# Layer 0's stacking transfers of a fused attention and expert kernel, split over two issuing engines

## The chip, the cores and the metric

The kernel runs on one core of one Trainium2 chip. Its engines are TensorE (PE), VectorE (DVE), ScalarE (ACT), GpSimd (POOL) and the sync engine (SP), each with a queue of its own that it takes in order; 16 DMA engines move data. The metric is the device time of one execution in microseconds; lower is better.

## The reference

Two layers on x (4 batches of 256 tokens, 128 wide) with a context (4 batches of 512 tokens, 96 wide). Each has cross-attention and a feed-forward part, both added to x after a layer norm. Layer 0's attention has 8 heads of 64:

```python
q = (x @ Wq).reshape(B, S, HEADS, DIM_HEAD).transpose(0, 2, 1, 3)
k = (context @ Wk).reshape(B, L, HEADS, DIM_HEAD).transpose(0, 2, 1, 3)
v = (context @ Wv).reshape(B, L, HEADS, DIM_HEAD).transpose(0, 2, 1, 3)
attn = jnp.einsum('bhsd,bhld->bhsl', q, k) * scale
attn = jax.nn.softmax(attn, axis=-1)
out = jnp.einsum('bhsl,bhld->bhsd', attn, v)
```

Its feed-forward part uses a fixed-point, piecewise linear gelu. Layer 1 has attention with 16 heads of 8 and a mixture of 8 experts, of which each token uses two.

## The kernel before, in words

Layer 0's attention goes batch by batch. Scores need near float32 accuracy at float16 speed, so each operand is kept as a high float16 part and a low one. For batch b, TensorE makes the projected keys (four matmuls "k0", one for each pair of heads) and queries ("q0", two) into banks of p_misc. ScalarE copies the high part into kx or qx (L1018, L1037), VectorE subtracts it from the bank for the low part (L755, L760) and gives the bank back. Each of kx and qx has one copy only, both parts of a batch beside each other.

Two heads lie one above the other in kx and qx. So that one matmul sums over 128 rows, "stack0" (L1250) moves them by transfers from SBUF to SBUF into kA, qA, kB and qB, views of a tile called region which have two buffers (b % 2): kA holds a head's high and low keys, qA its high queries twice, kB the high keys and qB the low queries. A batch takes six transfers of keys (256 KB each) and six of queries (128 KB each). The sync engine issues all twelve, in turn k k q q k k q q k q k q. It waits first for the keys' banks, before the first query transfer for the queries' banks, and from batch 2 on for the end of the scores of two batches back, whose buffer it overwrites. Each transfer adds 16 to one of kA_landed, qA_landed (one for even heads, one for odd), kB_landed, qB_landed.

Then TensorE makes "max" (a head's scores for its maximum, L468, reduced by VectorE at L766), "rows" (maxima transposed, L399, copied by ScalarE into mrow at L995, then by VectorE into qB at L780), "sc" (scores again, with the maxima taken off, L498; ScalarE's exponential at L1056 in two halves, each of which gives a bank back to the next head's scores) and "av" (values times probabilities, L517). "v0" is the projection of values, copied by ScalarE at L995; "ln", "xn" and "xT" are a layer norm's statistics, its result (VectorE, L729) and its transpose (TensorE, L399).

Before ScalarE overwrites kx or qx with the next batch, the old one must have left. It waits by stacked (L1003), which asks for all twelve transfers, in front of a batch's first key copy and its first query copy, and once more for layer 1, which uses kx and qx too.

The order of all steps is written out by schedule() (L65) as one list. Each engine walks the list and does its part of every kind that it knows; a kind that it doesn't know it passes. Around the change the list reads (kind, then batch and part or head; "stack0", b stands once for every batch):

- batch 0: q0 0 0, q0 0 1, **stack0 0**, split_w 1 (the weights' cast by ScalarE at L1001, the low part by VectorE at L744), cT 1, ln, v0 0 0, v0 0 1, xn, init 1, v0 0 2, v0 0 3, cT 2, cT 3, xT, max 0 0, k0 1 0, max 0 1, k0 1 1, ...
- batch 1: sc 0 1, max 0 5, q0 1 1, sum, max 0 6, **stack0 1**, sc 0 2, max 0 7, sum, init, sc 0 3, rows, k0 2 0, sum, av, max 1 0, k0 2 1, sc 0 4, sum, k0 2 2, ...
- batch 2: sc 0 7, max 1 5, sum, v0 1 0, av, max 1 6, ln, **stack0 2**, sc 1 0, v0 1 1, sum, max 1 7, av, rows, sc 1 1, v0 1 2, xT, xn, q0 3 0, ...
- batch 3: sc 1 7, y0, sum, av, max 2 6, **stack0 3**, sc 2 0, ln, sum, av, max 2 7, xn, sc 2 1, xT, up0, max 3 0, ...

Of the kernel before, what the change touches and what calls it, by code (L numbers as in the profile page):

```python
# [12 lines left out]
B = 4  # L13
# [213 lines left out]
def build(nc, t, out):  # L227
    ctx = ExitStack()
    with ctx:
        def sb(name, shape, dt=F32):  # L230
            return ctx.enter_context(nc.sbuf_tensor(name, shape, dt))

        def sem(name):
            return ctx.enter_context(nc.semaphore(name))

        def sems(name, n):
            return [sem(f"{name}{i}") for i in range(n)]
# [4 lines left out]
        cT = sb("cT", [CD, 2, B * C], F16)  # L242
# [22 lines left out]
        kA = region[:, 0:8192].rearrange("p (b h k) -> p b h k", b=2, h=H0)  # L265
        kB = region[:, 8192:16384].rearrange("p (b h k) -> p b h k", b=2, h=H0)
        qA = region[:, 16384:20480].rearrange("p (b h k) -> p b h k", b=2, h=H0)
        qB = region[:, 20480:24576].rearrange("p (b h k) -> p b h k", b=2, h=H0)
# [3 lines left out]
        kx = sb("kx", [P, 2, M0, C], F16)  # L272
        qx = sb("qx", [P, 2, M0, S], F16)
        v0 = sb("v0", [P, 2, KT, H0 * DH0])
# [8 lines left out]
        xT = sb("xT", [P, 2, S])  # L283
# [56 lines left out]
        kA_landed, qA_landed = sems("kA_landed", 2), sems("qA_landed", 2)  # L340
        kB_landed, qB_landed = sem("kB_landed"), sem("qB_landed")
# [3 lines left out]
        sc_full, sc_free = sems("sc_full", 2), sems("sc_free", 2)  # L345
# [25 lines left out]
        def misc_wait(eng, key):  # L371
            bank, use = misc[key]
            eng.wait_ge(misc_full[bank], use)
            return p_misc[:, bank, :], misc_free[bank]

        def misc_done(eng, key):

            bank, use = misc[key]
            eng.wait_ge(misc_free[bank], use)
# [3 lines left out]
        def head_number(layer, b, h):  # L383

            return b * H0 + h if layer == 0 else B * H0 + b * H1 + h
# [606 lines left out]
        def _(act):  # L992
# [7 lines left out]
                act.wait_ge(*((ld_wk0, 16) if n == 0 else (ld_wc, 48)))  # L1000
                act.copy(wc[:, 0, cols], wc_in[:, cols]).then_inc(wc_hi, 1)  # L1001

            def stacked(eng, batches):  # L1003
                for i in range(2):
                    eng.wait_ge(kA_landed[i], 32 * batches)
                    eng.wait_ge(qA_landed[i], 32 * batches)
                eng.wait_ge(kB_landed, 32 * batches)
                eng.wait_ge(qB_landed, 32 * batches)

            def context(b):  # L1010
                ps, _free = misc_wait(act, ("cT", b))
# [1 line left out]

            def keys0(b, m):
                if b and m == 0:
                    stacked(act, b)
                ps, _free = misc_wait(act, ("k0", b, m))
                act.copy(kx[:, 0, m, :], ps).then_inc(k_hi, 1)  # L1018

# [12 lines left out]

            def queries0(b, i):
                if b and i == 0:
                    stacked(act, b)
                ps, _free = misc_wait(act, ("q0", b, i))
                act.copy(qx[:, 0, 2 * i:2 * i + 2, :].rearrange("p m n -> p (m n)"), ps).then_inc(q_hi, 1)  # L1037

# [52 lines left out]
            def keys1(b):  # L1091

                if b == 0:
                    stacked(act, B)
                else:
                    act.wait_ge(k_bounced, 32 * b)
                ps, _free = misc_wait(act, ("k1", b))
                act.activation(kx[:, 0, 0, :], ps, ACT.Identity, bias=bk1[:, 0:1]).then_inc(k_hi, 1)

            def queries1(b):  # L1100
                if b == 0:
                    stacked(act, B)
                else:
                    act.wait_ge(q_bounced, 32 * b)
                ps, _free = misc_wait(act, ("q1", b))
                act.activation(qx[:, 0, 0, :], ps[:, 0:S], ACT.Identity, bias=bq1[:, 0:1]).then_inc(q_hi, 1)
# [9 lines left out]
            def activate(n, f):  # L1116
# [6 lines left out]
                if k:  # L1123
# [3 lines left out]
                    if last_n >= 2 and last_f == 0:  # L1127
                        act.wait_ge(y_full, last_n - 1)
                    act.copy(hh[:, last_n % 2, 0, last_f, :], hp[:, (k - 1) % 2, :]).then_inc(hh_done, 1)  # L1129

            steps = {"split_w": split_w, "cT": context, "k0": keys0, "v0": values0, "xT": xt, "q0": queries0, "rows": rows, "sc": softmax, "av": outputs,
                     "aT": heads_back, "up0": up0, "nodes": nodes_at, "k1": keys1, "q1": queries1, "aT1": heads_back1, "h1": up1,
                     "act": activate}
            for kind, *at in order:
# [98 lines left out]
        def _(sp):  # L1233
# [16 lines left out]
            def stack0(b):  # L1250


                def part(dst, src, i, low, landed):
                    sp.dma_start(dst[:, b % 2, i::2, :], src[64 * i:64 * i + 64, low, :, :]).then_inc(landed, 16)  # L1254

                for m in range(M0):
                    misc_done(sp, ("k0", b, m))
                if b >= 2:

                    sp.wait_ge(sc_full[1], head_number(0, b - 1, 0))  # L1260
                for i in range(2):
                    part(kA[0:64], kx, i, 0, kA_landed[i])
                    part(kA[64:128], kx, i, 1, kA_landed[i])
                    if i == 0:
                        for m in range(2):
                            misc_done(sp, ("q0", b, m))
                    part(qA[0:64], qx, i, 0, qA_landed[i])
                    part(qA[64:128], qx, i, 0, qA_landed[i])
                for i in range(2):
                    part(kB[0:64], kx, i, 0, kB_landed)  # L1270
                    part(qB[0:64], qx, i, 1, qB_landed)

            def bounce(b):

# [41 lines left out]
            def rest_of_weights(n):  # L1316
# [13 lines left out]
                sp.dma_start(f1b2[:, :], row(t["L1_xattn_b2"])).then_inc(ld_w2, 16)  # L1330

            steps = {"stack0": stack0, "zeros": zeros, "bounce": bounce, "stack1": stack1, "stage": stage_in, "init": rest_of_weights}
            for kind, *at in order:
                if kind in steps:
# [36 lines left out]
```

## Time and profile before

| | us |
|---|---|
| median of 3 runs | 501.96 (501.45 to 503.52) |
| the profiled execution | 501.99 |
| its span, first to last instruction | 500.3 |

| engine | busy us | share of the span |
|---|---|---|
| TensorE, matmuls | 436.3 | 87% |
| VectorE | 367.7 | 73% |
| ScalarE | 266.2 | 53% |
| GpSimd | 176.6 | 35% |

The mean granted clock of TensorE is 0.939 of full speed. The page also cuts the span into 40 equal slices of 12.5 us, each digit being tenths of a slice. Engines in the rows: PE is TensorE's matmul, PEld its weight load, DVE VectorE, ACT ScalarE, POOL GpSimd; SPq is the sync engine's queue, whose entries here are issues of transfers. Times count from the span's start. A timeline's row is: start, duration from the first to the last end of the merged instructions, engine, line, operation, output<-inputs, how many; in brackets the engine's idle time before it and what ended that. "p_misc L425" is a matmul of keys, and so on by the lines named above.

### The profile page before, as it was taken

How to read it: one execution, taken by the hardware profiler on the slowest of the kernel's cores; microseconds unless marked ns; L12 is line 12 of the kernel's file. 1: busy time of each engine (PE TensorE's matmuls, PEld its weight loads, DVE VectorE, ACT ScalarE, POOL GpSimd, SP SyncE). 2: the span in 40 equal slices, each digit the busy share in tenths (PEclk: the TensorE clock that was granted, in tenths of full speed). 3: DMA queues.
4: the chain of work that ended last, by engine and by line, in shares of the span. 5: the costliest groups of instructions: out<-in, count | busy, mean ns of one | idle time of the engine just before them, and what ended most of it. 6: DMA issues, size and time to landing. Idle time of an engine off the chain costs nothing.

```text
span 500.3 us, 8970 instructions
## 1 busy us (share of the span) xinstructions
PE 436.3 (87%) x3344; PEld 248.6 (50%) x3344; DVE 367.7 (73%) x718; ACT 266.2 (53%) x504; POOL 176.6 (35%) x205
## 2 busy tenths in 40 slices
PE   8569498997789968977985899999989999999996
PEld 3315154564356436544542544545546665656555
DVE  6855354555875799869986999882298888987775
ACT  3515253653824552456567376678755646465553
POOL 4218935427463492752426035710400104000000
PEclk9958698998979979997998899999999999999999
DMA  6664408007102005321142015400000000000000
GB/s 165 151 150 95 94 2 189 1 1 173 49 1 64 2 0 139 94 72 55 54 128 84 2 48 144 115 2 1 2 0 1 1 3 1 1 21 2 1 1 22
DMA packets 31487, 26.70 MB, mean 53 GB/s; under 512 B 4717, under 2 KB 28461, under 8 KB 31149
## 3 DMA queue, kind: packets, MB, share of 16 engines
q1 hardware_dynamic: 31445, 26.13, 20.9%
q8 instruction: 27, 0.44, 0.4%
q14 instruction: 15, 0.12, 0.1%
HBM read 12.10 MB, written 2.88 MB: 30 GB/s over the span
## 4 chain that ended last, share of the span: by engine, by line
PE 59%; DVE 22%; ACT 7%; issue 4%; SPq 3%; DMA 2%; POOL 2%; DVEq 0%; ACTq 0%; POOLq 0%
PE p_o L670 7%; PE p_sc L498 7%; PE p_misc L653 7%; PE p_sc L653 6%; PE p_misc L468 6%; DVE mx L766 6%; PE p_o L530 5%; PE p_o L517 4%; PE p_misc L399 4%; SPq L1254 3%; DVE xn L729 2%; DVE probs L953 2%; PE p_misc L425 2%; PE p_misc L562 2%; ACT probs L1122 2%
## 5 line engine op out<-in xcount | busy, mean ns | idle before, releaser
L766 DVE TENSOR_REDUCE mx<-p_misc 128x1 f32<-128x512 f32 x192 | 122.3, 684 | 20.4 <-PE p_misc L468 18.8
L1056 ACT ACTIVATE probs<-p_sc 128x512 f32<-128x512 f32 x192 | 104.6, 596 | 57.2 <-PE p_sc L498 56.9
L1122 ACT ACTIVATE probs<-p_misc 128x512 f32<-128x512 f32 x64 | 38.1, 597 | 56.6 <-PE p_sc L653 56.6
L953 DVE TENSOR_TENSOR probs<-probs,p_sc 128x512 f32<-128x512 f32 x64 | 44.0, 687 | 26.5 <-ACT probs L1122 24.7
L653 PE MATMUL p_misc<-qS,region 128*128 128x512 f16 x192 | 52.0, 380 | 3.8 <-DVE probs L953 2.6
L653 PE MATMUL p_sc<-qS,region 128*128 128x512 f16 x192 | 51.9, 379 | 0.0
L468 PE MATMUL p_misc<-kS,qS 96*128 96x512 f16 x128 | 40.6, 395 | 8.1 <-DVE mx L766 4.1
L1195 POOL TENSOR_TENSOR psums<-probs 128x256 f32<-128x256 f32 x32 | 26.0, 812 | 58.6 <-PE p_o L524 56.1
L1153 POOL TENSOR_SCALAR veps<-meanvar 128x2 f32<-128x2 f32 x16 | 3.7, 230 | 121.7 <-DVE meanvar L718 121.3
L670 PEld LDWEIGHTS p_o<-region,probs 128*128 128x128 f16 x720 | 42.7, 98 | 7.1
L670 PE MATMUL p_o<-region,probs 128*128 128x128 f16 x720 | 45.1, 219 | 0.0
L517 PE MATMUL p_o<-probs,v 128*64 128x256 f32 x256 | 38.3, 423 | 7.0 <-ACT probs L1056 7.0
L498 PE MATMUL p_sc<-qS,kS 128*128 128x256 f16 x256 | 40.6, 278 | 4.2 <-ACT probs L1056 3.9
L958 DVE TENSOR_TENSOR probs<-probs 128x512 f16<-128x512 f32 x64 | 43.8, 684 | 0.0
L530 PE MATMUL p_o<-probs,v 128*32 128x256 f32 x512 | 41.0, 398 | 0.0
L1129 ACT CAST probs<-probs 128x512 f16<-128x512 f32 x64 | 39.1, 611 | 1.4 <-DVE probs L953 1.4
L498 PE MATMUL p_sc<-region 128*128 128x256 f16 x256 | 36.6, 290 | 0.9 <-DVE region L780 0.9
L498 PEld LDWEIGHTS p_sc<-qS,kS 128*128 128x128 f16 x256 | 23.4, 98 | 19.8 <-ACT probs L1056 8.0
L498 PEld LDWEIGHTS p_sc<-region 128*128 128x128 f16 x256 | 25.7, 103 | 12.6 <-issue 3.6
L1213 POOL TENSOR_TENSOR region<-v,region 128x512 f16<-128x512 f32 x24 | 30.3, 1264 | 1.9
L653 PEld LDWEIGHTS p_sc<-qS,region 128*128 128x128 f16 x192 | 18.8, 98 | 22.7
L517 PEld LDWEIGHTS p_o<-probs,v 128*64 128x64 f32 x256 | 16.8, 146 | 24.7 <-issue 12.7
(163 smaller groups left out, 678.6 us busy)
## 6 DMA issues: line engine op xcount, KB each, us to landing
region<-kx SPq DMA_DIRECT2D x24, 256.0 KB, 3.9
v<-in_L_ffn_W_dram SPq DMA_DIRECT2D x24, 256.0 KB, 2.7
region<-qx SPq DMA_DIRECT2D x24, 128.0 KB, 3.9
kS<-kS SPq DMA_DIRECT2D x1, 1664.0 KB
kS<-k_scratch SPq DMA_DIRECT2D x8, 192.0 KB
k_scratch<-kx SPq DMA_DIRECT2D x4, 256.0 KB, 2.2
qS<-q_scratch SPq DMA_DIRECT2D x8, 96.0 KB
probs<-in_ctx_dram SPq DMA_DIRECT2D x1, 576.0 KB, 6.2
```

Source lines behind the costliest of these rows:

```text
L468: pe.matmul(ps, q[:, i * P:(i + 1) * P], k, start=True, stop=True).then_inc(full, 1)
L498: last = pe.matmul(p_sc[:, half, j * S:(j + 1) * S], k[:, kt * P:(kt + 1) * P], q, start=(i == 0), stop=(i == len(pairs) - 1))
L517: pe.matmul(p_o[64 * i:64 * i + 64, 0, m * S:(m + 1) * S], v0[:, b % 2, kt, h * DH0:(h + 1) * DH0], probs[:, h % 8, kt * S:(kt + 1) * S], ...
L530: last = pe.matmul(p_o[32 * j:32 * j + 32, n % 2, 0:S], v1[:, b % 2, c, h * VW:h * VW + 32], probs[:, h % 8, c * S:(c + 1) * S], start=(c ...
L653: last = pe.matmul(ps[:, f % 2, :], w[:, ws, e, f * P:(f + 1) * P], xh[:, xs, half * C:(half + 1) * C], start=(i == 0), stop=(i == 2))
L670: last = pe.matmul(p_o[:, n % 2, i * P:(i + 1) * P], hh[:, n % 2, hs, f, i * P:(i + 1) * P], ew[2][:, ws, e, f * P:(f + 1) * P], start=(at ...
L766: dve.tensor_reduce(mx[:, b % 2, i, h:h + 1], ps, AX_X, ALU.max).then_inc(free, 1)
L953: dve.tensor_tensor(hp[:, k % 2, :], sg[:, k % 2, :], p_sc[:, k % 2, :], ALU.mult).then_inc(hp_done, 1)
L958: dve.tensor_tensor(hh[:, n % 2, 1, f, :], hp[:, k % 2, :], hh[:, n % 2, 0, f, :], ALU.subtract).then_inc(hl_done, 1)
L1056: act.activation(probs[:, h % 8, half * 512:(half + 1) * 512], p_sc[:, half, :], ACT.Exp, scale=(DH0 if layer == 0 else DH1) ** -0.5).then ...
L1122: act.activation(sg[:, k % 2, :], p_misc[:, k % 2, :], ACT.Silu).then_inc(sg_done, 1)
L1129: act.copy(hh[:, last_n % 2, 0, last_f, :], hp[:, (k - 1) % 2, :]).then_inc(hh_done, 1)
```

## The change

The six query transfers of a batch are issued by ScalarE, at the place of "stack0" in ScalarE's own walk through the list, and the six key transfers still by the sync engine. ScalarE waits before them for the queries' two banks (VectorE's low parts), and from batch 2 on for the same scores as the sync engine. The sync engine no longer waits for the queries' banks. The wait for all twelve is split: before copies of keys ScalarE waits for the six key transfers, before copies of queries for the six query transfers. The number, shapes and sources of transfers stay the same.

```diff
-            def stacked(eng, batches):
+            def keys_stacked(batches):
                 for i in range(2):
-                    eng.wait_ge(kA_landed[i], 32 * batches)
-                    eng.wait_ge(qA_landed[i], 32 * batches)
-                eng.wait_ge(kB_landed, 32 * batches)
-                eng.wait_ge(qB_landed, 32 * batches)
+                    act.wait_ge(kA_landed[i], 32 * batches)
+                act.wait_ge(kB_landed, 32 * batches)
+
+            def queries_stacked(batches):
+                for i in range(2):
+                    act.wait_ge(qA_landed[i], 32 * batches)
+                act.wait_ge(qB_landed, 32 * batches)
+
+            def stack_queries(b):
+
+
+                def part(dst, i, low, landed):
+                    act.dma_start(dst[:, b % 2, i::2, :], qx[64 * i:64 * i + 64, low, :, :]).then_inc(landed, 16)
+
+                for m in range(2):
+                    misc_done(act, ("q0", b, m))
+                if b >= 2:
+                    act.wait_ge(sc_full[1], head_number(0, b - 1, 0))
+                for i in range(2):
+                    part(qA[0:64], i, 0, qA_landed[i])
+                    part(qA[64:128], i, 0, qA_landed[i])
+                for i in range(2):
+                    part(qB[0:64], i, 1, qB_landed)
...
             def keys0(b, m):
                 if b and m == 0:
-                    stacked(act, b)
+                    keys_stacked(b)
...
             def queries0(b, i):
                 if b and i == 0:
-                    stacked(act, b)
+                    queries_stacked(b)
...
             def stack0(b):
...
                 for i in range(2):
-                    part(kA[0:64], kx, i, 0, kA_landed[i])
-                    part(kA[64:128], kx, i, 1, kA_landed[i])
-                    if i == 0:
-                        for m in range(2):
-                            misc_done(sp, ("q0", b, m))
-                    part(qA[0:64], qx, i, 0, qA_landed[i])
-                    part(qA[64:128], qx, i, 0, qA_landed[i])
+                    part(kA[0:64], i, 0, kA_landed[i])
+                    part(kA[64:128], i, 1, kA_landed[i])
                 for i in range(2):
-                    part(kB[0:64], kx, i, 0, kB_landed)
-                    part(qB[0:64], qx, i, 1, qB_landed)
+                    part(kB[0:64], i, 0, kB_landed)
```

In keys1 and queries1 (layer 1) the same split is made, and ScalarE's table of kinds gets "stack0": stack_queries.

## Rows read from the trace of the kernel before

**Rows 1.** The page, busy time with its share, and TensorE in 40 slices.

```profile
PE 436.3 (87%) x3344; PEld 248.6 (50%) x3344; DVE 367.7 (73%) x718; ACT 266.2 (53%) x504; POOL 176.6 (35%) x205
...
PE   8569498997789968977985899999989999999996
```

**Rows 2.** ScalarE's waits, 14 to 130: us in total, times, longest.

```profile
ACT kx L1018 <- DMA region<-qx: 15.7, 2, 8.6
...
ACT qx L1037 <- DMA region<-qx: 4.2, 1, 4.2
```

**Rows 3.** Issues: timeline; then line L1254 in 14 to 30 (ns min/median/max, landing).

```profile
14.11 1.38 SPq L1254 DMA_DIRECT2D region<-kx  x2
...
17.90 1.48 SPq L1254 DMA_DIRECT2D region<-kx  x2
...
74.36 1.25 SPq L1254 DMA_DIRECT2D region<-kx  x2
...
78.01 1.44 SPq L1254 DMA_DIRECT2D region<-kx  x2
79.49 2.51 SPq L1254 DMA_DIRECT2D region<-qx  x2
...
L1254 SPq DMA_DIRECT2D region<-qx x6: 590/932/1402, 15.8 to 24.5; - x6
...
DMA to landing us min/median/max: 3.3/3.9/4.4
```

**Rows 4.** The timeline between 14 and 30.

```profile
14.92 0.83 ACT L1001 CAST wc<-probs 96x768 f16<-96x768 f32 x1
15.05 0.69 DVE L760 TENSOR_TENSOR qx<-p_misc,qx 128x512 f16<-128x512 f32 x1 [0.17 <-ACT qx L1037]
...
24.69 1.44 PE L425 MATMUL p_misc<-cT,wc 96*128 96x512 f16 x3
...
28.55 1.07 ACT L1018 CAST kx<-p_misc 128x512 f16<-128x512 f32 x2 [7.13 <-DMA region<-qx]
```

**Rows 5.** The timeline between 44 and 60.

```profile
44.53 0.69 DVE L760 TENSOR_TENSOR qx<-p_misc,qx 128x512 f16<-128x512 f32 x1
...
47.72 0.38 PE L399 MATMUL p_misc<-ident,mx 128*4 128x128 f32 x2 [1.12 <-DVE mx L766]
...
50.78 1.04 PE L498 MATMUL p_sc<-region 128*128 128x256 f16 x8
...
57.10 1.07 ACT L1018 CAST kx<-p_misc 128x512 f16<-128x512 f32 x2 [8.55 <-DMA region<-qx]
...
58.52 1.46 PE L425 MATMUL p_misc<-cT,wc 96*128 96x512 f16 x3 [6.70 <-DVE kx L755]
```

**Rows 6.** The timeline between 75 and 90.

```profile
75.39 0.58 ACT L995 COPY v<-p_misc 128x512 f32<-128x512 f32 x1 [0.38 <-PE p_misc L433]
...
80.80 0.36 ACT L995 CAST mrow<-p_misc 4x256 f16<-4x256 f32 x1 [1.75 <-PE p_misc L399]
...
83.41 0.44 PE L399 MATMUL p_misc<-ident,xn 128*128 128x128 f32 x2 [1.18 <-DVE xn L729]
...
88.50 0.58 ACT L1037 CAST qx<-p_misc 128x512 f16<-128x512 f32 x1 [4.25 <-DMA region<-qx]
```

**Rows 7.** The timeline between 112 and 123.

```profile
112.62 1.08 ACT L1056 ACTIVATE probs<-p_sc 128x512 f32<-128x512 f32 x2
...
121.81 0.44 PE L399 MATMUL p_misc<-ident,xn 128*128 128x128 f32 x2 [3.05 <-DVE xn L729]
```

**Rows 8.** Stretches: length, busy (instructions) PE PEld DVE ACT POOL; PEclk, DMA share, GB/s.

```profile
52.00:54.00 2.00, 0.00 (x0) 0.00 (x0) 0.00 (x0) 0.00 (x0) 1.74 (x4) 1.00 0.94 230
...
58.00:64.00 6.00, 5.47 (x20) 2.30 (x21) 5.07 (x9) 2.01 (x5) 5.57 (x4) 0.50 0.00 1
...
84.00:88.00 4.00, 3.69 (x13) 1.74 (x14) 0.00 (x0) 0.26 (x1) 0.00 (x0) 0.59 0.77 173
88.00:90.00 2.00, 2.00 (x9) 1.06 (x8) 0.69 (x1) 1.38 (x3) 0.00 (x0) 0.96 0.00 0
```

More of the change, by code:

```diff
@@ L1093, in keys1 @@
                 if b == 0:
-                    stacked(act, B)
+                    keys_stacked(B)
                 else:
@@ L1101, in queries1 @@
                 if b == 0:
-                    stacked(act, B)
+                    queries_stacked(B)
                 else:
@@ L1129, in activate @@
                     act.copy(hh[:, last_n % 2, 0, last_f, :], hp[:, (k - 1) % 2, :]).then_inc(hh_done, 1)
-            steps = {"split_w": split_w, "cT": context, "k0": keys0, "v0": values0, "xT": xt, "q0": queries0, "rows": rows, "sc": softmax, "av": outputs,
+            steps = {"split_w": split_w, "cT": context, "k0": keys0, "v0": values0, "xT": xt, "q0": queries0, "stack0": stack_queries, "rows": rows, "sc": softmax, "av": outputs,
                      "aT": heads_back, "up0": up0, "nodes": nodes_at, "k1": keys1, "q1": queries1, "aT1": heads_back1, "h1": up1,
@@ L1250, in stack0, with part @@
             def stack0(b):
-                def part(dst, src, i, low, landed):
-                    sp.dma_start(dst[:, b % 2, i::2, :], src[64 * i:64 * i + 64, low, :, :]).then_inc(landed, 16)
+                def part(dst, i, low, landed):
+                    sp.dma_start(dst[:, b % 2, i::2, :], kx[64 * i:64 * i + 64, low, :, :]).then_inc(landed, 16)
                 for m in range(M0):
```

## The prediction

> **What bounds the kernel now.** I read the page's shares and slices first [rows 1]: TensorE is busy 87% of the span, but its slices have digits of 4 to 6 only in the first third, where layer 0 stacks its four batches. The change touches that part alone, so what counts is who lets TensorE stand there. The view of ScalarE's waits says it [rows 2]: copies of keys waited 15.7 us in two places for a query transfer, and a copy of queries 4.2 us in one. The timeline then shows what each of the three is worth.
>
> *Batch 0's stacking.* ScalarE copies batch 1's first keys at 28.55 after 7.13 us of waiting, though TensorE had made them by 24.69 + 1.44 = 26.13 [rows 4]. *Batch 1's.* ScalarE waits 8.55 us, up to 57.10, TensorE 6.70 us with it, and TensorE restarts at 58.52 [rows 5]. It then works at a granted clock of 0.50 up to 64 [rows 8], that is at 1.2 GHz and no longer at 2.4, after having stood idle, so the gap costs more than its length. *Batch 2's.* ScalarE waits 4.25 us for the copy of queries at 88.50 [rows 6], but TensorE is 3.69 us of 4 busy meanwhile [rows 8]; little hangs on it. *Batch 3's.* No copy waits for a transfer; TensorE stands 3.05 us before 121.81 for a normalisation by VectorE [rows 7].
>
> **What six issues cost on ScalarE.** This is the term that decides. For every batch ScalarE gets six query transfers to issue, ahead of work already queued behind them. It issues none in this trace, so the nearest rows are the sync engine's [rows 3]. One query issue takes 0.590 us at least, 1.402 at most. On an empty queue the first go fast and a later one drags; I read that as a queue that takes the next transfer only when an early one is through, but the rows show the durations and not the reason. The first six issues of a batch lasted from 14.11 to 17.90 + 1.48 = 19.38, and from 74.36 to 78.01 + 1.44 = 79.45: 5.27 and 5.09 us. I take I = 5.3 us for six on ScalarE. The lower end is six at 0.59: 3.5 us. For the upper end: two engines would send at once, and the DMA engines are already 77 to 94% busy in such stretches [rows 8]. If the third query transfer lands only when the seventh of twelve does now (issued 79.49, 3.9 us to landing, so 83.4), the sixth issue ends there, 7.4 us after a start at 75.97. An end below zero is excluded: the issues come on top of all that ScalarE has.
>
> The Trainium skill (DMA: Bandwidth & Descriptors, section "Issuing engines are not separate DMA queues") says that transfers of several issuers run on the same 16 engines, and that spreading them saves only the issue time, usually small beside the transfer. The trace speaks against "small" here: six issues fill over 5 us where one transfer lands in 3.9. Were they small on ScalarE too, the second rival below would come true.
>
> **Batch 0.** ScalarE now casts weights at 14.92. With the change it first waits for VectorE's low part of the queries (15.05 + 0.69 = 15.74), issues from about 15.8, and is free at 15.8 + I = 21.1. Behind the issues stand that cast, the context's copy, the copies of values, two more contexts and x transposed. VectorE's low parts and TensorE's value matmuls take each from it in turn, up to the key matmul that ends at 26.13 [rows 4]. All of it shifts by 21.1 − 14.92 = 6.2 us, and the first key copy comes at 32.3, not at 28.55: +3.8 us. The keys' own transfers limit nothing any more (six issues end near 19.4 and land near 23). With I = 3.5 or 7.4 it is +2.0 or +5.9. The clock adds a term of unknown sign: TensorE stands longer before the value matmuls, may do these at half clock, and may be back at full clock earlier afterwards. A low stretch of 5.47 us busy in six [rows 8] costs 2.7 us at most; I allow a third of it as a loss (+1.0), half as a gain (−1.5), and take −0.5. Batch 0: +3.3 us, from +0.5 to +6.9.
>
> **Batch 1.** The queries' low part is done at 44.53 + 0.69 = 45.22. ScalarE is held to 45.3 + I = 50.6; behind it stand the exponentials of heads 2 and 3, the row copy and the first key copy of batch 2. TensorE can't make head 3's scores before head 2's exponential gives its bank back. From 50.6 on there are 0.6 for half an exponential, 1.04 for scores, and the work that now runs from 47.72 to 50.78 + 1.04 = 51.82, 4.1 us, and 0.5 of hand-overs: 6.3 us, so TensorE is at 56.9 where it is at 58.52 now [rows 5]. The keys' transfers have landed before the copy (their six issues need 5.3 us from 41.5, and 3.9 to landing: 50.1; the copy comes near 54). Of the 6.7 us gap the change gives back 1.6 us; the rest is the same gap in another place, with its half clock. With I = 3.5 it gives 3.4, with 7.4 it costs 0.5. Batch 1: −1.6 us.
>
> **Batch 2.** ScalarE is free for the issues at 75.39 + 0.58 = 75.97 and held to 81.3. An exponential of two halves (1.08) and a value copy (0.58) stand between them and the row copy, now at 80.80, which comes at 83.0 then. From it, 83.41 − 80.80 = 2.6 us lead through VectorE's row and normalisation to TensorE's transposes: 85.6 and not 83.41, +2.2 us [rows 6]. The wait that ends at 88.50 goes; I put 0.5 us on it, since TensorE lacked only 0.31 of 4 us in its course. Nothing slack follows: TensorE is busy 2.00 of 2 us after 88 [rows 8]. Batch 2: +1.7 us, from −0.1 to +4.3.
>
> **Batch 3.** ScalarE is held from 112.62 + 1.08 = 113.70 to 119.0. Its next exponential and then scores follow, from 119.6 to 120.6, before 121.81, and the normalisation that TensorE awaits there takes nothing from the delayed work [rows 7]. Zero; with I = 7.4 the scores end at 122.7 and it costs 0.9.
>
> On the sync engine six issues go from ahead of the weights of later stages, which nobody awaits yet, and its waits for queries go too. Nothing.
>
> **Sum.** The profiled execution took 501.99 us around a span of 500.3; the median of the runs is 501.96, so either is the base. 3.3 − 1.6 + 1.7 + 0 = +3.4: **505.4 us**. With all low ends: 0.5 − 3.4 − 0.1 = −3.0, 499.0. With all high ends: 6.9 + 0.5 + 4.3 + 0.9 = +12.6, 514.6.
>
> **The rivals.**
> *Issues cost their bare 0.59 us.* Each queue gets half of the transfers and never fills. 2.0 − 0.5 − 3.4 − 0.1 = −2.0: 500.0, no change. For it: the first issues of a batch are that short. Against it: the sync engine's sixth ends after 5.1 to 5.3 us in two batches, with a queue that began empty [rows 3].
> *Issues don't hold ScalarE's work (faster).* If each holds it for under 0.25 us (batch 0's break-even: 28.55 − 26.13 = 2.4 gained, less 15.8 − 14.92 = 0.9 lost, over six), the waits of [rows 2] simply end. About −2 in batch 0; in batch 1 the gap of 6.7 us with most of its half clock, 2.7 at most; −0.5 in batch 2. Together −11: 491. Against it: no issue in [rows 3] is under 0.59 us, and an engine takes its queue in order. For it: these rows are another engine's.
> *Two streams contend badly.* I near 7.4 in every batch: +9 to +13, about 513. The DMA engines' 77 to 94% speak for some of this.
>
> **Chances.** Forecast, with I from 4.5 to 6.5, 0.58; bare issues 0.17; free issues 0.15; contention 0.10. 0.5% (2.5 us) is about what a measurement of this kernel can tell from no change. Slower: nine tenths of the forecast's and all of contention's, 0.63. Same: the rest of the forecast's and most of the bare issues', 0.21. Faster: 0.16. The range that leaves out no more than 2 in 10 drops the free issues and the worst of contention: 498.5 to 512.5.
>
> **What would show each step.** ScalarE's queue has six issues a batch that last 5.3 us together; the weights' cast starts near 21 and not at 14.92; no copy of keys waits for a query transfer; the 6.7 us gap before 58.5 becomes one of about 5 us before head 3's scores; the row copy now at 80.80 is 2 us later against its surroundings; the gap before 121.81 stays. The prediction is wrong if ScalarE's issues are short, or long with its computing going on beside them: then time falls. It is wrong in size if the clock's low stretches grow or vanish.

## The result and the profile after

The changed kernel takes 518.08 us (median of 4, 517.33 to 518.5) against 502.57 for the kernel before beside it: ratio 1.0281, 95% interval 1.0244 to 1.0318. The forecast was 505.4 within 498.5 to 512.5: the direction was right, 15.5 us of loss stand against 3.4, and the range missed the time. The profiled execution took 518.31 us around a span of 516.5.

The page of the kernel after: TensorE's slices, which answer to [rows 1], the queues, and the chain by engine.

```profile
PE   8177496998577987896998589999989999999996
...
q1 hardware_dynamic: 24917, 22.99, 17.9%
q10 hardware_dynamic: 6528, 3.15, 3.2%
...
PE 59%; DVE 21%; ACT 8%; ACTq 6%; issue 4%; DMA 1%; SPq 0%; DVEq 0%
```

q10 is the new queue with the query transfers. ACTq, ScalarE's queue, holds 6% of the chain that ends last, where the sync engine's issues had 3% before. ScalarE's waits in 14 to 150, which answer to [rows 2] (us in total, times, longest):

```profile
ACT probs L1075 <- issue: 25.8, 3, 9.5
...
ACT kx L1037 <- PE p_misc L425: 9.6, 7, 2.4
...
ACT wc L1001 <- issue: 9.1, 1, 9.1
```

The waits for transfers have gone, all 19.9 us of them (15.7 + 4.2). In their place stand 34.9 us behind its own issues (25.8 + 9.1). The timeline shows the four, each with the work behind it; these rows answer to [rows 4 to 7]:

```profile
15.84 8.28 ACTq L1017 DMA_DIRECT2D region<-qx  x6
24.16 0.83 ACT L1001 CAST wc<-probs 96x768 f16<-96x768 f32 x1 [9.13 <-issue]
...
51.23 6.98 ACTq L1017 DMA_DIRECT2D region<-qx  x6
58.31 1.09 ACT L1075 ACTIVATE probs<-p_sc 128x512 f32<-128x512 f32 x2 [7.89 <-issue]
...
80.51 8.79 ACTq L1017 DMA_DIRECT2D region<-qx  x6
89.41 1.08 ACT L1075 ACTIVATE probs<-p_sc 128x512 f32<-128x512 f32 x2 [8.39 <-issue]
...
123.03 9.97 ACTq L1017 DMA_DIRECT2D region<-qx  x6
133.11 1.08 ACT L1075 ACTIVATE probs<-p_sc 128x512 f32<-128x512 f32 x2 [9.51 <-issue]
```

And TensorE, each time ahead of the next head's scores (the last shows why [rows 7]'s cover didn't hold):

```profile
58.97 1.89 PE L498 MATMUL p_sc<-region 128*128 128x256 f16 x8 [7.37 <-ACT probs L1075]
...
90.06 1.89 PE L498 MATMUL p_sc<-region 128*128 128x256 f16 x8 [4.34 <-ACT probs L1075]
...
133.76 1.89 PE L498 MATMUL p_sc<-region 128*128 128x256 f16 x8 [5.98 <-ACT probs L1075]
```

Where the time came from is read from events that both traces have: ScalarE's first row copy, and its copies of finished heads out of p_o (osb), of which each batch has two in layer 0.

| event | before | after | shift | added since the event above |
|---|---|---|---|---|
| first row copy | 35.99 | 41.82 | 5.8 | batch 0's issues: +5.8 |
| 1st osb copy | 72.41 | 77.44 | 5.0 | batch 1's: −0.8 |
| 2nd | 93.43 | 103.32 | 9.9 | batch 2's: +4.9 |
| 3rd | 111.68 | 121.57 | 9.9 | 0 |
| 4th | 133.82 | 148.98 | 15.2 | batch 3's: +5.3 |
| 5th | 157.87 | 174.38 | 16.5 | +1.3, at a lower clock (below) |
| 24th | 359.53 | 375.73 | 16.2 | −0.3 |

### The profile page after: what moved, and what is told of

The parts are those of the page before. It is cut to its first block, busy times and chain, and to the rows that moved or that the text cites. A ratio compares the mean times of both kernels' runs of the same rounds, so it can differ in the third digit from the quotient of the medians.

```text
span 516.5 us, 8962 instructions
## 1 busy us (share of the span) xinstructions
PE 438.5 (85%) x3344; PEld 251.2 (49%) x3344; DVE 368.3 (71%) x718; ACT 266.4 (52%) x504; POOL 176.4 (34%) x205
## 4 chain that ended last, share of the span: by engine, by line
PE 59%; DVE 21%; ACT 8%; ACTq 6%; issue 4%; DMA 1%; SPq 0%; DVEq 0%
PE p_sc L498 8%; PE p_o L670 7%; PE p_misc L653 6%; ACTq L1017 6%; PE p_sc L653 6%; PE p_misc L468 6%; DVE mx L766 6%; PE p_o L530 5%; PE p_o L517 4%; PE p_misc L399 4%; PE p_misc L433 2%; DVE probs L953 2%; PE p_misc L562 2%; DVE xn L729 2%; PE p_misc L425 2%
## 5 line engine op out<-in xcount | busy, mean ns | idle before, releaser
L498 PE MATMUL p_sc<-region 128*128 128x256 f16 x256 | 38.3, 300 | 18.6 <-ACT probs L1075 17.7
```

The costliest lines, as they stand in the source:

```text
L498: last = pe.matmul(p_sc[:, half, j * S:(j + 1) * S], k[:, kt * P:(kt + 1) * P], q, start=(i == 0), stop=(i == len(pairs) - 1))
```

## The experiments

Two questions were open: does holding ScalarE explain the loss, and why did six issues take 7 to 10 us and not 5.3? Medians of the kernel before, measured beside the experiments, were 503.7 to 504.8, so ratios and traces are compared, not bare times. Each trace is of one execution.

**Holding ScalarE without giving it an issue.** The sync engine issues all twelve transfers as before, the wait for the twelve is split as in the change, and at the place of the issues ScalarE waits for four query transfers.

```diff
+            def hold(b):
+                for i in range(2):
+                    act.wait_ge(qA_landed[i], 32 * (b + 1))
...
-            steps = {..., "q0": queries0, "rows": rows, ...
+            steps = {..., "q0": queries0, "stack0": hold, "rows": rows, ...
```

> The kernel before with the split waits; the sync engine issues all twelve transfers in the old order and ScalarE none. But where ScalarE issued in the changed kernel it now waits for the first four query transfers to land. By the rows of before (issue and 3.9 us) that frees it at 24.6, 52.7, 84.6 and 123.2, against 24.2, 52.5, 84.5 and 123.1 in the changed kernel (its times less the shift that it has by then). Theory (all the loss comes from ScalarE's being held, none from the transfers): batches cost about +6, -1, +5 and +5 us, total 514 to 520 on a base of 502 to 505, ratio 1.024 to 1.034. Rival (two streams on the DMA engines, later landings, cost most of it): ratio under 1.012.

Measured: 515.76 us, within the 514 to 520 expected, and ratio 1.0238 (1.0178 to 1.0298), just under the 1.024 expected and well over the rival's 1.012. ScalarE's waits in this kernel, 14 to 150:

```profile
ACT probs L1063 <- DMA region<-qx: 26.5, 3, 9.5
...
ACT wc L1001 <- DMA region<-qx: 9.3, 1, 9.3
```

They are the changed kernel's waits (25.8 and 9.1) with another cause. The 24th osb copy stands at 373.19, 13.7 us later than before, of 16.2 in the changed kernel. So holding ScalarE makes 13.7 of the 16.2 us by itself, with no issue on it and one stream of transfers. Part of the rest goes with a difference in the clock, which no run sets by itself: in both kernels TensorE restarts at half clock after batch 2's gap, but here (restart at 91.06) it was back within 94 to 96, and in the changed kernel (90.06) only within 97 to 99. Stretches (length, busy time with instructions of PE, PEld, DVE, ACT, POOL, then clock, DMA share, GB/s), first of this kernel, then of the changed one, each about 3 to 5 and 5 to 7 us after the restart:

```profile
94.00:96.00 2.00, 1.48 (x7) 0.91 (x5) 0.00 (x0) 0.86 (x2) 0.00 (x0) 0.78 0.00 0
...
96.00:98.00 2.00, 2.00 (x14) 0.98 (x13) 0.69 (x1) 0.59 (x1) 0.00 (x0) 1.00 0.00 0
```

```profile
93.00:95.00 2.00, 1.48 (x5) 0.97 (x4) 0.00 (x0) 0.86 (x2) 0.00 (x0) 0.50 0.00 0
...
95.00:97.00 2.00, 2.00 (x7) 0.98 (x8) 0.02 (x1) 0.58 (x1) 0.00 (x0) 0.50 0.00 0
```

**Queries issued alone.**

```diff
             def stack0(b):
...
+                for i in range(2):
+                    sp.wait_ge(qA_landed[i], 32 * (b + 1))
+                sp.wait_ge(qB_landed, 32 * (b + 1))
                 for i in range(2):
                     part(kA[0:64], i, 0, kA_landed[i])
```

> The changed kernel, but the sync engine starts a batch's key transfers only when its query transfers have landed, so that ScalarE's six issues meet no other stacking traffic. Read ScalarE's issue entries in batches 1, 2 and 3 (batch 0 has the last loads beside it), not the total, which the later keys lengthen. Theory contention (each issue is held up until an early transfer is through, and the key transfers on the same DMA engines slow that down): the six fall from 6.98, 8.79 and 9.97 us to 4.3 to 5.3 us, and one transfer lands 3 to 4 us after its issue, not 6. Theory ScalarE's issues are dear in themselves (about 1.4 us each on this engine): they stay at 8 to 10 us. Theory bare issues: 3.5 us.

The line of the issues in 80 to 96, of the changed kernel and then of this one (ns min/median/max):

```profile
L1017 ACTq DMA_DIRECT2D region<-qx x6: 618/1512/1842, 80.5 to 87.7; - x6
...
DMA to landing us min/median/max: 4.8/6.1/6.4
```

```profile
L1017 ACTq DMA_DIRECT2D region<-qx x6: 609/646/652, 83.0 to 86.3; - x6
...
DMA to landing us min/median/max: 2.4/2.5/2.6
...
82.96 3.99 ACTq L1017 DMA_DIRECT2D region<-qx  x6
```

Alone, six issues take 4.0 us in every batch, nearly the bare price, with nothing that drags; that is even less than the 4.3 to 5.3 us that the theory gave them. ScalarE's issues aren't dear, and six queries don't fill their own queue. The keys' transfers beside them make them slow. (Its one execution took 511.4 us, in which the shorter hold and the later keys are mixed.)

**Three issues on ScalarE, three behind the keys.**

```diff
             def stack_queries(b):
...
-                for i in range(2):
-                    part(qA[0:64], i, 0, qA_landed[i])
-                    part(qA[64:128], i, 0, qA_landed[i])
-                for i in range(2):
-                    part(qB[0:64], i, 1, qB_landed)
+                part(qA[0:64], 0, 0, qA_landed[0])
+                part(qA[64:128], 0, 0, qA_landed[0])
+                part(qA[0:64], 1, 0, qA_landed[1])
...
             def stack0(b):
...
                 for i in range(2):
                     part(kB[0:64], i, 0, kB_landed)
+                for m in range(2):
+                    misc_done(sp, ("q0", b, m))
...
+                rest(qA[64:128], 1, 0, qA_landed[1])
+                for i in range(2):
+                    rest(qB[0:64], i, 1, qB_landed)
```

> The changed kernel, but ScalarE issues three of a batch's six query transfers and the sync engine the other three behind its six keys. Theory (ScalarE is held because its queue takes a fourth transfer only when the first is through): three issues last 1.9 to 2.2 us, and the total is 494 to 500. Rival (a price per transfer of 1.4 us each, whatever stands in the queue): 4.2 us, total 502 to 506.

(`rest` is `part` on the sync engine.) Measured: 501.01 us, ratio 0.9934 (0.9912 to 0.9956), between the theory's total and the rival's. The theory of the issues fell here: with three transfers in its own queue nothing should drag, yet three took 3.62 to 4.17 us. The rival gave 4.2 us, but its price of 1.4 us whatever stands in the queue is refuted by the 0.65 us above. Timeline of this kernel:

```profile
71.83 7.68 SPq L1271 DMA_DIRECT2D region<-kx  x6
72.94 4.16 ACTq L1017 DMA_DIRECT2D region<-qx  x3
```

**Issues behind the keys.** ScalarE first waits for four keys' landing.

```diff
                 for m in range(2):
                     misc_done(act, ("q0", b, m))
+                for i in range(2):
+                    act.wait_ge(kA_landed[i], 32 * (b + 1))
```

> The changed kernel, but ScalarE issues a batch's queries only when four of its six key transfers have landed: the sync engine has issued all six by then and has two, about 2.4 us of data, in flight. Read ScalarE's entries, not the total, which the waiting lengthens. Theory A (an issue is slow because the other engine issues at the same time): all six take 0.6 to 0.65 us, 4.0 us together, as they do alone. Theory B (an issue is slow because the DMA engines are busy with transfers already issued): the second and third take 1.2 us or more, 5.2 us or more together.

Six took 4.29 us in batch 0, 3.97 in batch 1 and 608 to 650 ns each in batch 2 (521.68 us in one execution): theory A, it seemed, with two transfers in flight doing no harm. But another reading fits too, that few transfers are in flight by then. The next run parts the two.

**Small transfers beside the queries.** To the kernel with queries alone it adds, ahead of the sync engine's new waits:

```diff
+                for m in range(2):
+                    misc_done(sp, ("q0", b, m))
+                for i in range(6):
+                    sp.dma_start(small[:, i, :, :], kx[0:64, 0, :, 0:16]).then_inc(small_landed, 16)
+                sp.wait_ge(small_landed, 96 * (b + 1))
```

> The kernel in which ScalarE's six queries are issued alone (0.60 to 0.68 us each, 4.0 us together), with one thing added: beside them the sync engine issues six transfers of as many pieces as a key transfer but 32 bytes each, so almost no data. Their result isn't used. Read the entries of both engines, not the total. Theory A (issuing from two engines at once is itself shared and slow): ScalarE's issues take 1.2 to 1.4 us from the second on, 7 us or more together. Theory B (an issue waits for room among transfers in flight of both queues, and it is the data of the keys, 1.2 us each, that keeps the room taken): they stay at 0.65 us, 3.9 to 4.5 us together.

(`small` is a tile of its own.) In its four batches ScalarE's six took 4.14 to 4.39 us (514.46 us in one execution). Timeline of this kernel, batch 3, where both engines issue side by side:

```profile
122.94 4.14 ACTq L1019 DMA_DIRECT2D region<-qx  x6
123.47 3.98 SPq L1285 DMA_DIRECT2D small<-kx  x6
```

Theory A is out: twelve issues from two engines run at nearly full pace when half of them, of as many pieces, move almost nothing. So it is the keys' data that slows ScalarE's issues, across the two queues, and six key transfers beside them do it where two in flight don't. Theory B's room among the transfers in flight, shared by both queues and kept taken by that data, fits every run; that such a room is the mechanism, and how much there is of it, no run shows.

**The split of the waits alone, and with the keys first.** The first keeps the sync engine's order; the second changes it to keys first:

```diff
                     part(kA[0:64], kx, i, 0, kA_landed[i])
                     part(kA[64:128], kx, i, 1, kA_landed[i])
-                    if i == 0:
-                        for m in range(2):
-                            misc_done(sp, ("q0", b, m))
+                for i in range(2):
+                    part(kB[0:64], kx, i, 0, kB_landed)
+                for m in range(2):
+                    misc_done(sp, ("q0", b, m))
+                for i in range(2):
                     part(qA[0:64], qx, i, 0, qA_landed[i])
                     part(qA[64:128], qx, i, 0, qA_landed[i])
                 for i in range(2):
-                    part(kB[0:64], kx, i, 0, kB_landed)
                     part(qB[0:64], qx, i, 1, qB_landed)
```

> The kernel before, with the second half of the change alone: copies of keys wait for the six key transfers, copies of queries for the six query transfers; the sync engine issues all twelve in the old order, in which the last key transfer is the eleventh. Theory: the two key waits end one transfer earlier, 0.7 to 1.3 us each, and the total falls by 0 to 2 us, ratio 0.996 to 1.000. Rival (the split does harm by itself): above 1.005.

> As the split waits alone, and the sync engine issues a batch's six key transfers first and its six query transfers behind them; ScalarE issues nothing. Theory (the waits for transfers were real, only ScalarE was the wrong place to pay for them): in batch 0 the key copy at 28.55 comes at 26 to 27, in batch 1 the one at 57.10 comes at 50 to 51, TensorE's 6.7 us gap nearly closes, and the clock doesn't fall there; the first maxima wait for queries 1 to 3 us more. Total 491 to 495, ratio 0.977 to 0.986. Rival (the queries' landing takes the place of the keys'): same as before, 0.995 to 1.005.

Measured: the split alone 503.8 us, 0.9977 (0.9952 to 1.0002); no harm, and no gain that can be told from none. Its trace has the key copies at 27.46 and 55.82, not at 28.55 and 57.10, but its stacking began 0.48 us earlier too (first issue at 13.63, not 14.11). Keys first: 497.67 us, 0.9859 (0.9836 to 0.9882). Timeline of the latter, batch 1's stretch:

```profile
46.76 4.54 SPq L1257 DMA_DIRECT2D region<-qx  x6
...
50.71 0.59 ACT L1021 CAST kx<-p_misc 128x512 f16<-128x512 f32 x1 [2.23 <-DMA region<-kx]
...
51.89 1.01 PE L468 MATMUL p_misc<-region 128*128 128x512 f16 x2 [2.19 <-issue]
```

The wait of 8.55 us [rows 5] is 2.23 now and TensorE's 6.70 is 2.19: the waits were real, and an order on one queue removes most of them. The queries behind six keys take 4.54 us to issue, on an engine with no computing behind them. It gained 7.1 us where about 10 were expected (491 to 495 us in total). The clock still falls at the restart, against the expectation: the two matmuls above take 1.01 us, not 0.60. And the first maxima come later: TensorE stands 2.19 us here and 3.18 us before 25.52. The profile names no releaser for these ("issue"); by the timing the queries' landing is what it lacks.

**The same issues on ScalarE, spread.** Two at the old place, then one after each of ScalarE's next four steps. `pending` holds the issues that are still to be made; stack_queries fills it and makes the first.

```diff
             for kind, *at in order:
                 if kind in steps:
                     steps[kind](*at)
+                    if pending:
+                        pending.pop(0)()
```

> The changed kernel, but ScalarE issues two of a batch's six query transfers at the old place and one behind each of its next four steps. Theory (ScalarE is held by each issue, 1.3 to 2.0 us while the keys' issues run beside it and 0.65 us alone): the last issues fall beside idle time or behind the keys, and the total is between the kernels: 504 to 511, ratio 1.003 to 1.015. Rival (the whole of the holding is on the path wherever it stands): ratio 1.025 to 1.03.

Measured: 497.87 us, 0.986 (0.9826 to 0.9894): faster than before, where the theory gave 504 to 511 us and the rival more, so both missed. Five of batch 2's six issues still take 1.4 to 1.75 us, but each holds only the next step, and part of ScalarE's idle time takes them up. At the 1st osb copy it is 7.1 us ahead of the kernel before (65.31, before 72.41).

**The queries on GpSimd.** stack_queries as in the change, with pool for act.

> The changed kernel, but GpSimd issues the six query transfers of a batch at the same place in the order, ScalarE none. There are two issuing engines again, and ScalarE is free. Theory (the holding of ScalarE is the loss): the waits for transfers shrink as the change meant and the total is 492 to 500, ratio 0.98 to 0.995, less what GpSimd's later sums cost. Rival (two streams contend, whoever issues): ratio above 1.01. No row shows what an issue takes on GpSimd.

Measured: 505.85 us, 1.0032 (1.0004 to 1.0061): neither. GpSimd's six take 3.7 to 3.9 us, and up to the 1st osb copy (64.94) it gains 7.5 us, as the theory says. Then GpSimd's own queue is what is held: its issues for batch 2 come at 79.08 only, behind sums and a layer norm's step, and in batch 3 they (116.14 to 119.79) stand themselves ahead of such a step, for which TensorE waits 7.0 us. TensorE's waits in this kernel, 14 to 150:

```profile
PE p_misc L399 <- DVE xn L729: 13.5, 3, 7.0
```

**Spread for batches 0 and 1, keys first on the sync engine for 2 and 3.** Both edits above, chosen by b.

> ScalarE's issues spread over its steps, as in the kernel with the spread issues, but for batches 0 and 1 only; for batches 2 and 3 the sync engine issues six keys and then six queries, as in the kernel with the keys first. In the traces, from the end of one group of heads to the end of a later one, batch 2's stretch took 22.8 us with spread issues and 20.9 with keys first, batch 3's 22.3 either way, batches 0 and 1 together 65.3 and 66.6. Theory (the batches' costs add up): 1.9 us less than with all issues spread, 494.5 to 497.5, ratio 0.979 to 0.985. Rival (a later stretch takes the gain back): ratio 0.985 to 0.99.

Measured: 496.39 us, 0.9854 (0.9818 to 0.989); the interval spans the theory's range and the rival's, so it decides for neither. Batches 2 and 3 took 20.92 and 22.07 us, as expected. The trace shows what the rival said: 1.2 us ahead of the kernel with all issues spread at the 4th osb copy (127.45, there 128.65), this kernel has lost it all by the 12th (281.78, there 281.70). With the same gap of TensorE behind it (0.95 us, at 254.38 here, at 255.88 there), it goes on at half clock, the other at full:

```profile
255.50:257.00 1.50, 1.50 (x5) 0.98 (x5) 0.02 (x1) 0.00 (x0) 1.32 (x2) 0.56 0.00 1
257.00:258.50 1.50, 1.50 (x13) 0.51 (x10) 0.00 (x0) 1.46 (x4) 1.36 (x3) 0.50 0.00 0
```

```profile
257.00:258.50 1.50, 1.50 (x12) 1.00 (x15) 0.02 (x1) 0.55 (x2) 1.30 (x2) 1.00 0.02 7
258.50:260.00 1.50, 1.50 (x13) 0.88 (x6) 0.00 (x0) 1.26 (x3) 1.36 (x3) 1.00 0.01 4
```

(The first fence is this kernel, the second the one with all issues spread.) The two and the keys-first kernel, 496.4 to 497.9 us, all beat both kernels of the case and can't be told apart.

## Why the prediction was wrong

**The reading of the profile was right**, and so was the way to the loss: ScalarE's issues hold the cast, exponentials and row copies queued behind them, and TensorE's gap moves and doesn't close. Two steps failed.

**The main step that failed is "What six issues cost on ScalarE".** It took I = 5.3 us from the sync engine's first six issues. Measured were 8.28, 6.98 and 8.79 us, and in batch 3 9.4 from the exponential's end (122.52 + 1.08 = 123.60) to 133.0. With these in place of 5.3 the prediction's own formulas give: batch 0, free at 24.1, a shift of 9.2, +6.8 − 0.5 = +6.3 (measured +5.8); batch 1, 45.3 + 7.0 + 6.3 = 58.6 against 58.52, +0.1 (−0.8); batch 2, row copy at 75.97 + 8.8 + 1.66 = 86.4, +5.6 − 0.5 = +5.1 (+4.9); batch 3, scores end at 113.7 + 9.4 + 0.6 + 1.04 = 124.7, +2.9 (+5.3). The sum is +14.4 against 15.2 at the 4th osb copy. That it comes so near is in part luck: batches 0 to 2 come out 1.6 us too dear and batch 3 2.4 us too cheap.

**Why it was mis-sized.** 5.3 us was the price of a queue that has keys and queries in turn and the DMA engines to itself, and I gave the drag to the queue's own filling. The three issues that took 4 us refute that. The drag is the keys' data: alone six queries cost 4.0 us, below the value taken; beside the keys 7.0 to 9.4. The rows hinted at it: the DMA engines were 77 to 94% busy [rows 8], and the twelve transfers took 14 us from the first issue to the last landing (74.36 to 84.6 + 3.9). I used that for the upper end alone (7.4 us), and that end was low too: with two queues a query transfer of batch 2 lands 6.1 us after its issue, not 3.9. What happened is the contention rival, to which I gave 0.10, and by more than its own +9 to +13. I also set six issues against the landing of one transfer (over 5 us against 3.9); one against one it is 0.6 to 1.4 against 3.9, which is small. What costs is that several stand in a row in front of work.

**The bare-issue and the free-issue rivals** are out: ScalarE's issues took 0.6 to 2.05 us, and none let its later work go ahead. **Batch 3's zero** fell with the size: the cover of 3.05 us was named, with the point from which it is gone. **Zero for the sync engine's side** held as far as the runs tell: the split of waits by itself can't be told from no change (0.9977, 0.9952 to 1.0002).

**The second step that failed is the clock**, which was allowed −1.5 to +1.0 around batch 0 and nothing later. In batch 0 the −0.5 had the right sign: the granted clock was 0.50 in 24 to 40 before and 0.87 in 26 to 40 after. In batch 3 the gap now ends at 133.76, and TensorE then works at half clock for 8 us; the kernel before had its gap of 3.05 us there and was back at full clock within 126 to 128. The stretches, after, then before:

```profile
134.00:142.00 8.00, 7.48 (x24) 4.69 (x24) 1.29 (x2) 3.21 (x8) 0.00 (x0) 0.50 0.25 46
```

```profile
122.00:126.00 4.00, 3.54 (x10) 2.35 (x10) 0.75 (x2) 1.21 (x3) 0.47 (x1) 0.57 0.92 210
...
126.00:128.00 2.00, 2.00 (x16) 1.05 (x14) 0.96 (x2) 1.07 (x3) 0.00 (x0) 1.00 0.07 14
```

The scores took 1.89 us and not 1.04, and from the transposes behind them to the next head's scores it is 7.49 us (135.44 to 142.93) where it was 5.96 (121.81 to 127.77): 0.85 + 1.5, which is the 2.4 us that the formulas lack in batch 3. Between the 4th and 5th osb copies the changed kernel lost 1.3 us more. After a gap of the same 1.85 us the shift is 14.9 us (149.86, now 164.74), at the 5th copy 16.5, and the granted clock was 1.00 in 147 to 155 before and is 0.79 in 162 to 170. So some 3.7 us of the loss stand in stretches of lower clock. No experiment set the clock by itself, so it isn't shown as their cause.

## What to carry to other kernels

Price an issue that is moved to a computing engine by what else is in flight when it is made, not by its own duration: here, beside another engine's transfers, six issues held ScalarE for 7.0 to 9.4 us, and alone for 4.0. Before moving issues to another engine, sort the ones that the critical wait needs to the front of the queue that exists; here that, with a wait for those alone, gave 7 us. If issues must stand on a computing engine, put one behind each step and not six in a row: the same twenty-four cost 15.5 us in blocks, and spread out the kernel was 6.4 us faster than before.

## What the runs showed of the hardware

- The sync engine's transfers slow ScalarE's issues, though each has a queue of its own: an issue of 0.65 us alone takes up to 2.05 us beside six transfers of 256 KB in the changed kernel (2.16 in the one with three on ScalarE), and 0.9 us at most beside six of as many pieces of 32 bytes. GpSimd's six weren't slowed: 3.90 us in batch 0 (from 16.40), beside the sync engine's key issues of 14.12 to 20.80.
- Two streams moved the same twelve transfers no faster. In batch 2 it is 14.1 us from the first issue to the last landing with one issuer (74.36 to 88.5) and 13.1 to 14.7 with two (79.4, and a last issue at 87.7 with 4.8 to 6.4 to its landing); what changed was how long a query transfer takes from its issue to its landing, 2.5 us alone, 3.9 in one queue, 6.1 in two.
- TensorE's granted clock after a gap isn't the same from trace to trace. With equal work and a gap of 0.95 us it stayed at 1.0 in one and fell to 0.5 (1.2 GHz) in another, worth about 1.6 us (10.4 or 12.0 us between the 11th and 12th osb copies). Executions of one kernel differ in it too: 13 of the kernel before had a mean granted clock of 0.931 to 0.949 and took 501.4 to 507.1 us. So 1 to 2 us between two traces need not come from what was changed.
